# Diagonal blocks computed once, their decay and shift on GpSimd, and the attention result kept transposed

## The chip, the cores and the metric

The kernel runs on one core of a Trainium2 chip. The metric is the device time of one execution in microseconds (us); three runs before the change gave 2750.56, 2752.46 and 2753.69 us. Everything is computed in float32 or in sums of bf16 parts; the tensor engine has two clock levels, and a window of the profile shows the granted one as a share of full speed (1.00 or 0.50).

## The reference

The reference is one transformer block on x of 8 x 1024 x 256, with a modulated layer norm ahead of attention and ahead of the feed-forward part. Cut to what matters here:

```python
q, k, v = h @ W_q, h @ W_k, h @ W_v
latent = (k + v) @ W_down_kv                      # 64 wide
k_rec, v_rec = latent @ W_up_k, latent @ W_up_v   # 16 heads of 16
scores = einsum("bhqd,bhkd->bhqk", qh, k_rec) / sqrt(256)
scores = scores * exp(-0.01 * abs(t[:, None] - t[None, :]))
attn = softmax(scores)
x = x + ga * (einsum("bhqk,bhkd->bhqd", attn, v_rec) @ W_o)
h = layernorm(x) * (1 + cb) + sb
x = x + gb * fp4_linear(silu(fp4_linear(h, w_gate)) * fp4_linear(h, w_up), w_down)
```

fp4_linear rounds both operands, in blocks of 16, to a grid of eight magnitudes and multiplies.

## The kernel before

The kernel has five stages: a small setup, the projections, attention (lines 492 to 968), a setup of the feed-forward part, and the feed-forward part (lines 1137 to 1481). The change touches attention and the last stage.

**The decay.** The decay of the distance between query and key is split into two factors, one for the query's row and one for the key's, each with its own sign of the exponent. So there are two versions of the queries and keys: "low" serves keys at or behind the query in one direction, "up" the other. Each float32 value is held as three bf16 parts; a product of two such values is six products of parts, stacked along the contraction (96 rows), and three more rows carry the negated maximum of the query (KROWS 96, ROWS 99), so that a product comes out of TensorE already shifted for the exponential. In a block of 128x128 on the diagonal both versions are needed, each on its side.

**Units and steps.** A unit is one batch and four heads; there are 32. It has 16 steps g: half hf = g // 8 of the queries (512 of them) against key block kb = g % 8 (128 keys). Steps 0 to 3 and 12 to 15 hold the diagonal (`is_diagonal`). In a step TensorE computes, for each of four heads, one tile of 128 keys by 512 queries in one of two score banks (`scores`, L702 to L724), and between them the score tiles of a later unit whose row maxima VectorE takes (`max_tile` L681, `maxima` L850; the custom instruction at L856 multiplies by the decay and takes the maximum). ScalarE takes the exponential of each tile (L817). At the end of the step TensorE multiplies the probabilities of step g - 2 with the values, which have a column of ones for the sum (`values`, L738 to L752). A score bank is free when the exponential two tiles back is done.

**The diagonal before.** In a diagonal step the score tile's diagonal 128 columns come from the low version (L718), and a product of the identity with a mask of -2^100 (`unserved`, L719) takes away the wrong side. Behind the second head TensorE computes the four up blocks into side_ps (`up_diagonals`, L734). VectorE limits them with a mask (`limit_up`, L891), ScalarE takes their exponential in the next step (L821), and GpSimd adds them to the probabilities (`add_diagonal`, L651). TensorE's `values` of the step wait for that.

**The output before.** ScalarE copies the accumulated output out of PSUM (L812, at steps 1 and 9), TensorE turns it by four transposes (`turn_out`, L762, at steps 5 and 10), VectorE inverts the sums and multiplies (L914, L920), and GpSimd's queue stores it (L657).

**The maxima.** At steps 7 and 8 VectorE splits the maxima of the next unit into three parts (`split_maxima`, L860 to L876); TensorE turns them at step 9 (L699), VectorE copies them (L881), and SyncE writes them into the three extra rows of the queries (`load_max_rows`, six DMAs, L600).

**Queues.** SyncE runs in the order of `step` (L603 to L612): it waits until all exponentials of a unit are done (L607), then issues 24 loads of the low queries and keys two units on and the up ones of the next unit (L487), the values (L593), and, once the maxima are turned, their rows.

**The last stage** runs 64 tiles of 128 tokens through a software pipeline (L1143 to L1151): attention is loaded, turned by TensorE (`turn_attention`, L1266), copied by ScalarE together with the turned normed input (L1317), projected (L1239), normed, rounded, multiplied with gate and up (L1284), rounded again, turned, and multiplied down (L1249). GpSimd raises one column a tile to the power -0.5 there (L1362), as it does four columns a half batch in the projections (L339).

## Time and profile before

| what | us |
|---|---|
| median of three runs | 2752.46 |
| the profiled execution | 2753.01 |
| its span in the trace | 2751.1 |
| TensorE busy (share) | 2592.5 (94%) |
| VectorE busy | 2308.7 (84%) |
| ScalarE busy | 1600.6 (58%) |
| GpSimd busy | 971.2 (35%) |

The span is the stretch from the first to the last instruction in the trace; the execution's own time has 1.9 us around it. A busy time is the sum of the times in which the engine had an instruction running. Matmuls are pipelined, so the distance between the starts of two of them tells what one costs. Projections take about the first 350 us, attention the time from there to 2060, the last stage the time from 2105 on. The mean granted clock is 0.944.

### The profile page before, as it was taken

Reading aid. Unit: us, or ns where it says so; the run is one execution under the profiler, and the core shown is the slowest. Engines: PE = TensorE matmul, PEld = TensorE weight load, DVE = VectorE, ACT = ScalarE, POOL = GpSimd, SP = SyncE. Lnnn points to the kernel's source line nnn. Section 1 sums busy time; section 2 is a strip of 40 time slices with the busy share of each in tenths; the row PEclk is TensorE's granted clock in tenths of the full one; section 3 lists DMA queues with packets and bytes.
Section 4 is the critical chain, followed back from the end, with each engine's and each line's share of the span. In section 5 each row is a group of like instructions: output and inputs, shape, how many; then the busy total and the mean of one; then the engine's idle time right before and its main releaser. Section 6 shows DMA issues by size and latency. Waiting matters only on the chain. (4 is left out here: it accounts for less than half of the span.)

```text
span 2751.1 us, 44454 instructions
## 1 busy us (share of the span) xinstructions
PE 2592.5 (94%) x15110; PEld 1205.3 (44%) x15110; DVE 2308.7 (84%) x4659; ACT 1600.6 (58%) x2988; POOL 971.2 (35%) x865
## 2 busy tenths in 40 slices
PE   5787669999999999999999999999977999999998
PEld 3333304344344344344344344343323566666665
DVE  5988788888888888888888888888755888888886
ACT  3666507777777777777777777777762222222221
POOL 3666532222122122122122122122131565556664
PEclk9667659999999999999999999999996999999999
DMA  4778864546546536446446446456201111111110
GB/s 153 239 243 257 264 127 82 85 62 91 82 62 92 81 66 95 74 69 96 72 71 95 70 74 95 69 74 92 47 7 39 37 44 42 41 41 43 41 34 18
DMA packets 207074, 238.20 MB, mean 87 GB/s; under 512 B 32256, under 2 KB 150784, under 8 KB 206720
## 3 DMA queue, kind: packets, MB, share of 16 engines
q1 hardware_dynamic: 194560, 218.56, 41.2%
q0 software_dynamic: 3072, 8.39, 1.2%
q10 hardware_dynamic: 9216, 8.39, 0.9%
q8 instruction: 122, 2.00, 0.4%
q14 instruction: 104, 0.85, 0.1%
HBM read 149.79 MB, written 83.89 MB: 85 GB/s over the span
## 5 line engine op out<-in xcount | busy, mean ns | idle before, releaser
L856 DVE CUSTOM_DVE_ANT_0 unread<-max_ps,toeplitz_sb 128x1024 bf16<-128x1024 f32 x1024 | 1218.5, 1218 | 212.9 <-PE max_ps L689 207.6
L817 ACT ACTIVATE probs<-score_ps 128x512 f32<-128x512 f32 x2048 | 1111.5, 598 | 431.0 <-PE score_ps L722 287.3
L689 PE MATMUL max_ps<-k_low,q_low 96*128 96x512 bf16 x2048 | 712.9, 391 | 27.5 <-DVE ident_bf L847 17.9
L651 POOL TENSOR_TENSOR probs<-probs,up_probs 128x512 f32<-128x512 f32 x256 | 336.3, 1314 | 610.0 <-ACT up_probs L821 610.0
L750 PE MATMUL pv_ps<-probs,v 128*32 128x512 f32 x4096 | 545.5, 605 | 3.3 <-POOL probs L651 3.3
L714 PE MATMUL score_ps<-q_up,k_up 99*128 99x512 bf16 (+3 forms) x1280 | 408.6, 320 | 5.3 <-ACT probs L817 4.5
L722 PE MATMUL score_ps<-q_low,k_low 99*128 99x512 bf16 (+3 forms) x1280 | 406.2, 318 | 5.2 <-ACT probs L817 4.5
L1284 PE MATMUL gu_ps<-wgu_t,turned 128*128 128x512 f32 (+1 forms) x768 | 314.4, 559 | 0.6 <-DVE hid L1445 0.6
L657 POOL DMA_DIRECT2D attn<-out_n x64 | 48.8, 763 | 694.8 <-DVE out_n L920 671.4
L714 PEld LDWEIGHTS score_ps<-q_up,k_up 99*128 99x128 bf16 x1280 | 123.8, 97 | 357.3 <-ACT probs L817 340.8
L689 PEld LDWEIGHTS max_ps<-k_low,q_low 96*128 96x128 bf16 x2048 | 193.3, 99 | 146.0 <-DVE row_max L856 68.3
L719 PE MATMUL score_ps<-unserved,ident_bf 128*128 128x128 bf16 x1024 | 225.8, 220 | 0.0
L718 PE MATMUL score_ps<-q_low,k_low 99*128 99x128 bf16 x1024 | 224.7, 219 | 0.8 <-ACT probs L817 0.7
L346 POOL TENSOR_TENSOR parts<-rest,parts 128x512 bf16<-128x512 f32 x128 | 172.8, 1369 | 110.3 <-ACT parts L461 108.7
L1284 PEld LDWEIGHTS gu_ps<-wgu_t,turned 128*128 128x128 f32 x768 | 141.7, 191 | 141.0 <-issue 124.0
L722 PEld LDWEIGHTS score_ps<-q_low,k_low 99*128 99x128 bf16 x1280 | 126.0, 99 | 164.3 <-ACT probs L817 149.9
L1249 PE MATMUL fdown_ps<-wd_g,hid_t 128*128 128x256 f32 (+1 forms) x768 | 190.7, 390 | 4.6 <-DVE y_out L1459 3.4
L1324 ACT ACTIVATE silu<-gu_ps 128x704 f32<-128x704 f32 x64 | 48.6, 759 | 248.7 <-PE gu_ps L1284 248.7
L891 DVE TENSOR_TENSOR up_probs<-side_ps,up_limit 128x512 f32<-128x512 f32 x256 | 175.6, 686 | 13.8 <-PE side_ps L734 11.4
L1317 ACT ACTIVATE turned<-fturn_ps 128x512 f32<-128x512 f32 (+1 forms) x68 | 39.0, 573 | 233.8 <-PE fturn_ps L1274 221.8
L821 ACT ACTIVATE up_probs<-up_probs 128x512 f32<-128x512 f32 x256 | 162.1, 633 | 0.0
L1249 PEld LDWEIGHTS fdown_ps<-wd_g,hid_t 128*128 128x128 f32 (+1 forms) x768 | 141.3, 191 | 44.9 <-issue 26.3
(145 smaller groups left out, 3186.3 us busy)
## 6 DMA issues: line engine op xcount, KB each, us to landing
splits<-parts SPq DMA_DIRECT2D x128, 384.0 KB, 2.7
q_low<-splits SPq DMA_DIRECT2D x192, 128.0 KB, 4.4
k_low<-splits SPq DMA_DIRECT2D x192, 128.0 KB, 7.2
q_up<-splits SPq DMA_DIRECT2D x192, 128.0 KB, 9.8
k_up<-splits SPq DMA_DIRECT2D x192, 128.0 KB, 12.7
v_padded<-v_out SPq DMA_DIRECT2D x64, 256.0 KB, 3.7
v<-v_padded SPq DMA_DIRECT2D x32, 512.0 KB, 14.8
x_in<-in_L_attn_x SPq DMA_DIRECT2D x16, 512.0 KB, 5.3
```

What stands on the lines that cost most here:

```text
L651: nc.gpsimd.tensor_tensor(probs[:, g % PROBS, :, at:at + P], probs[:, g % PROBS, :, at:at + P], up_probs[:, g % 2], ALU.add).then_inc(diag ...
L689: mm = pe.matmul(max_ps[:, i % 2, half * HALF:(half + 1) * HALF], low[0][u][0:KROWS, h, qb * P:(qb + 1) * P], low[1][u][0:KROWS, h, half * ...
L714: mm = pe.matmul(score_ps[:, i % 2, 0:turn - q0], up[1][u % 2][:, h, ks], up[0][u % 2][:, h, q0:turn], start=True, stop=True)
L718: pe.matmul(at, low[1][u][:, h, ks], low[0][u][:, h, ks], start=True, stop=False)
L719: mm = pe.matmul(at, ident_bf[:], unserved[:], start=False, stop=True)
L722: mm = pe.matmul(score_ps[:, i % 2, turn - q0:HALF], low[1][u][:, h, ks], low[0][u][:, h, turn:q1], start=True, stop=True)
L750: mm = pe.matmul(pv_ps[h * VW:(h + 1) * VW, :], v[u][:, kb, h, :], probs[:, g % PROBS, h, :], start=(kb == 0), stop=(kb == TILES - 1))
L817: nc.scalar.activation(probs[:, g % PROBS, h, :], score_ps[:, i % 2, :], ACT.Exp).then_inc(exp_done, 1)
L856: nc.vector.tensor_tensor_reduce(unread[:, i % 2, :], max_ps[:, i % 2, :], toeplitz[:, at:at + S], 1.0, -3.0e38, ALU.mult, ALU.max, row_ma ...
L891: nc.vector.tensor_tensor(up_probs[:, g % 2], side_ps[:], up_limit[:].unsqueeze(1).broadcast_to([P, UH, P]), ALU.min).then_inc(up_limited, 1)
L1249: mm = pe.matmul(down_ps[:, 0:D], hid_t[i % 2][0:rows, c, :], w["wd_g"][0:rows, b, c, :], start=(c == 0), stop=(c == IC - 1))
L1284: mm = pe.matmul(gu_ps[:, c:min(c + HALF, GU)], turned[(i + TURN_INPUT) % 2][:, DC + k, :], w["wgu_t"][:, k, c:min(c + HALF, GU)], start=( ...
```

## The change

In attention each diagonal block is computed once, from the low version without the maximum rows, into side_ps, one step ahead of its own step (`diagonals`); the score tile leaves its 128 columns out. ScalarE copies the four blocks out (`copy_diagonal`), GpSimd multiplies them with a decay (`decay_diagonal`) and subtracts the query maxima (`shift_diagonal`), and ScalarE takes the exponential into the probabilities in the step after (`diagonal_exp`). The maxima for that are turned whole, in float32, beside the three parts, stored to DRAM and loaded back broadcast over the 128 partitions, 1 MB a half unit (`load_shift`). The mask, `limit_up`, `add_diagonal` and the up blocks go.

The values' padding columns are all ones, so 16 rows of the accumulated output hold the sum. It is not turned: SyncE copies these rows beside the output's by four DMAs (`move_sums`), GpSimd raises a tile of 128x512 to the power -1 and multiplies (`normalise`, both halves after the next unit's step 3), and SyncE stores it by four DMAs (`store_out`). The last stage loads it transposed and has no `turn_attention`. The values and the buffers of the weights' rounding share less memory than before.

```diff
@@ attention, SyncE
+        def load_shift(unit, hf):
+            sp.wait_ge(max_stored, 16 * (unit + 1))
+            if unit > 0:
+                sp.wait_ge(diag_shifted, 2 * DIAG * (unit - 1) + DIAG * (hf + 1))
+            sp.dma_start(shift[:, hf], t["max_whole"].rearrange("(h c) q -> h (c q)", c=TILES)[
+                :, hf * HALF:(hf + 1) * HALF].unsqueeze(0).broadcast_to([P, UH, HALF])).then_inc(shift_loaded[hf], 16)
+
+        def move_sums(unit, hf):
+            n = 2 * unit + hf
+            sp.wait_ge(out_copied, n + 1)
+            if unit > 0:
+                sp.wait_ge(out_normal, n - 1)
+            for h in range(UH):
+                sp.dma_start(inverse[h * VW:h * VW + HD, hf, :],
+                             out_t[h * VW + HD:(h + 1) * VW, n % OUTS, :]).then_inc(sums_moved[hf], 16)
+
+        def store_out(b, u, hf):
+            n = 2 * (UNITS * b + u) + hf
+            sp.wait_ge(out_normal, n + 1)
+            for h in range(UH):
+                sp.dma_start(t["attn_t"][b, u * UH + h, :, hf * HALF:(hf + 1) * HALF],
+                             out_t[h * VW:h * VW + HD, n % OUTS, :]).then_inc(out_stored[n % OUTS], 16)
         def step(b, u, last):
...
             if not (last and u == UNITS - 1):
                 load_up(b if u < UNITS - 1 else b + 1, (u + 1) % UNITS)
+            if unit > 0:
+                load_shift(unit, 1)
+                sp.wait_ge(pv_done, STEPS * unit)
+            if not (last and u == UNITS - 1):
+                load_v(b if u < UNITS - 1 else b + 1, (u + 1) % UNITS)
+            if unit > 0:
+                move_sums(unit - 1, 1)
+                store_out(*before, 0)
+                store_out(*before, 1)
+            move_sums(unit, 0)
+            if not (last and u == UNITS - 1):
                 load_max_rows(unit + 1, (u + 1) % UNITS)
+                load_shift(unit + 1, 0)
@@ attention, GpSimd
+        def decay_diagonal(unit, g):
+            n = diagonals_before(unit, g)
+            pool.wait_ge(diag_copied, n + 1)
...
+            nc.gpsimd.tensor_tensor(diag[:, g % 2], diag[:, g % 2], diag_decay[:].unsqueeze(1).broadcast_to([P, UH, P]),
+                                    ALU.mult).then_inc(diag_decayed, 1)
+
+        def shift_diagonal(unit, g):
+            n, hf, at = diagonals_before(unit, g), g // TILES, g % DIAG * P
+            pool.wait_ge(diag_decayed, n + 1)
+            pool.wait_ge(shift_loaded[hf], 16 * (unit + 1))
+            nc.gpsimd.tensor_tensor(diag[:, g % 2], diag[:, g % 2], shift[:, hf, :, at:at + P],
+                                    ALU.subtract).then_inc(diag_shifted, 1)
+
+        def normalise(unit, hf):
+            n = 2 * unit + hf
...
+            pool.wait_ge(sums_moved[hf], 16 * UH * (unit + 1))
+            nc.gpsimd.tensor_tensor(inverse[:, hf, :], inverse[:, hf, :], minus_one[:].broadcast_to([P, HALF]),
+                                    ALU.pow).then_inc(inverted, 1)
+            pool.wait_ge(inverted, n + 1)
+            nc.gpsimd.tensor_tensor(out_t[:, n % OUTS, :], out_t[:, n % OUTS, :], inverse[:, hf, :],
+                                    ALU.mult).then_inc(out_normal, 1)
+
+        def unit_steps(unit):
             for g in range(DIAG):
-                add_diagonal(b, u, g)
+                decay_diagonal(unit, g)
+                shift_diagonal(unit, g)
+            if unit > 0:
+                normalise(unit - 1, 0)
+                normalise(unit - 1, 1)
             for g in range(TILES + DIAG, STEPS):
-                add_diagonal(b, u, g)
+                decay_diagonal(unit, g)
+                shift_diagonal(unit, g)
@@ attention, TensorE
+            pe.transpose(turned_max, max_parts[:].rearrange("p t n -> p (t n)"), ident_bf[:])
+            pe.transpose(turned_whole, row_max[:, unit % 2], w["ident"][:]).then_inc(max_turn_ready, 1)
...
             if is_diagonal(g):
-                at = score_ps[:, i % 2, turn - q0:turn - q0 + P]
-                pe.matmul(at, low[1][u][:, h, ks], low[0][u][:, h, ks], start=True, stop=False)
-                mm = pe.matmul(at, ident_bf[:], unserved[:], start=False, stop=True)
                 turn += P
...
             for h in range(UH):
-                mm = pe.matmul(side_ps[:, h, :], up[1][u % 2][:, h, ks], up[0][u % 2][:, h, ks],
+                mm = pe.matmul(side_ps[:, h, :], low[1][u][0:KROWS, h, ks], low[0][u][0:KROWS, h, ks],
                                start=True, stop=True)
...
-                    if h == 1 and is_diagonal(g):
-                        up_diagonals(b, u, g)
+                    if h == 1 and is_diagonal((g + 1) % STEPS) and not (last and g == STEPS - 1):
+                        diagonals(*steps_on(b, u, g))
@@ attention, ScalarE
         def exp(unit, g, h):
             i = UH * g + h
+            first = P if is_diagonal(g) and g % DIAG == 0 else 0
+            end = HALF - P if is_diagonal(g) and g % DIAG == DIAG - 1 else HALF
...
+            nc.scalar.activation(diag[:, g % 2], side_ps[:], ACT.Copy).then_inc(diag_copied, 1)
...
+            act.wait_ge(diag_shifted, diagonals_before(unit, g + 1))
+            nc.scalar.activation(probs[:, g % PROBS, :, at:at + P], diag[:, g % 2], ACT.Exp).then_inc(diag_exp_done, 1)
...
                 for h in range(UH):
                     exp(unit, g, h)
-                    if h == UP_EXP and not (first and g == 0) and is_diagonal((g - 1) % STEPS):
-                        up_exps(*steps_back(b, u, g, 1))
+                    if h == DIAG_EXP and not (first and g == 0) and is_diagonal((g - 1) % STEPS):
+                        diagonal_exp(*steps_back(b, u, g, 1))
+                if is_diagonal((g + 1) % STEPS) and not (last and g == STEPS - 1):
+                    copy_diagonal(*steps_on(b, u, g))
@@ attention, VectorE: limit_up, invert_sums and normalise go; copy_turned copies the whole maxima too
+            nc.vector.tensor_copy(max_whole[:], turned_whole).then_inc(max_turn_copied, 1)
@@ last stage
-            sp.dma_start(attn_in[i % 4][:], t["attn"][b, i * P:(i + 1) * P, :]).then_inc(tile_loaded[i % 4], 16)
+            sp.dma_start(attn_in[i % 4][:], t["attn_t"][b, :, :, tokens].rearrange(
+                "(k h) d s -> (h d) k s", k=DC)).then_inc(tile_loaded[i % 4], 16)
...
-                mm = pe.matmul(out_ps[:, 0:D], turned[i % 2][:, k, :], w["wo_g"][:, b, k, :],
+                mm = pe.matmul(out_ps[:, 0:D], attn_in[i % 4][:, k, :], w["wo_g"][:, b, k, :],
```

## Rows read from the trace of the kernel before

**Rows 1.** Windows of attention and feed: busy us (count), PEclk, DMA share, GB/s

```profile
1000.00:1050.00 50.00, 50.00 (x374) 20.59 (x366) 43.36 (x81) 37.73 (x73) 11.79 (x10) 1.00 0.47 69
2300.00:2700.00 400.00, 399.90 (x1577) 257.26 (x1575) 354.42 (x995) 91.27 (x165) 241.18 (x249) 1.00 0.13 39
```

**Rows 2.** Timeline of the SyncE queue: start us, us, engine, line, operation

```profile
1012.23 1.78 SPq L600 DMA_DIRECT2D q_low<-max_turned  x3
...
1029.20 2.65 SPq L487 DMA_DIRECT2D q_low<-splits  x6
...
1040.34 0.43 SPq L593 DMA_DIRECT2D v<-v_padded  x1
...
1080.60 3.01 SPq L487 DMA_DIRECT2D q_low<-splits  x6
```

**Rows 3.** Timeline of TensorE in one unit

```profile
1005.62 1.07 PE L750 MATMUL pv_ps<-probs,v 128*32 128x512 f32 x8
...
1008.57 1.06 PE L750 MATMUL pv_ps<-probs,v 128*32 128x512 f32 x8
...
1012.65 0.66 PE L762 MATMUL side_ps<-ident_sb,out_t 128*128 128x128 f32 x4
1013.14 0.38 PE L722 MATMUL score_ps<-q_low,k_low 99*128 99x512 bf16 x1
...
1016.08 0.23 PE L718 MATMUL score_ps<-q_low,k_low 99*128 99x128 bf16 x1
1016.14 0.22 PE L719 MATMUL score_ps<-unserved,ident_bf 128*128 128x128 bf16 x1
...
1018.40 1.06 PE L750 MATMUL pv_ps<-probs,v 128*32 128x512 f32 x8
...
1021.73 1.06 PE L750 MATMUL pv_ps<-probs,v 128*32 128x512 f32 x8
```

**Rows 4.** Timeline of ScalarE in a diagonal step

```profile
1020.92 0.63 ACT L821 ACTIVATE up_probs<-up_probs 128x512 f32<-128x512 f32 x1
1021.44 1.09 ACT L817 ACTIVATE probs<-score_ps 128x512 f32<-128x512 f32 x2
```

**Rows 5.** GpSimd groups by form: count | busy us, mean ns | idle

```profile
L651 POOL TENSOR_TENSOR probs<-probs,up_probs 128x512 f32<-128x512 f32 x256 | 336.3, 1314 | 610.0 <-ACT up_probs L821 610.0
...
L1362 POOL TENSOR_TENSOR rstd<-var_eps,minus_half 128x1 f32<-128x1 f32 x64 | 42.4, 662 | 31.9 <-DVE var_eps L1421 31.9
...
L339 POOL TENSOR_TENSOR rstd<-var_eps,minus_half 128x4 f32<-128x4 f32 x16 | 16.2, 1010 | 20.9 <-DVE var_eps L274 20.8
```

**Rows 6.** Timeline of projection: GpSimd and VectorE

```profile
118.77 2.57 POOL L346 TENSOR_TENSOR parts<-rest,parts 128x512 bf16<-128x512 f32 x2
...
120.36 1.53 DVE L303 TENSOR_TENSOR rest<-full,parts 128x512 f32<-128x512 f32 x1
...
125.86 0.68 DVE L303 TENSOR_TENSOR rest<-full,parts 128x512 f32<-128x512 f32 x1
```

**Rows 7.** Windows at attention's start and under a unit's loads

```profile
404.00:410.00 6.00, 4.90 (x10) 0.66 (x10) 5.81 (x11) 0.00 (x0) 0.00 (x0) 0.50 1.06 336
419.00:422.00 3.00, 2.62 (x25) 1.58 (x26) 3.00 (x6) 2.79 (x6) 1.16 (x1) 1.00 1.07 219
1030.00:1050.00 20.00, 20.00 (x158) 8.85 (x155) 17.02 (x29) 15.96 (x32) 6.43 (x5) 1.00 1.08 147
```

**Rows 8.** Timeline of TensorE at the end of attention

```profile
2062.50 5.62 PE L1047 MATMUL wmod_ps<-wmod_hi,silu_c 128*8 128x512 f32 x8 [4.28 <-PEq L968]
```

**Rows 9.** Timeline of TensorE in a feed tile

```profile
2412.24 0.44 PE L1266 MATMUL fturn_ps<-ident_sb,attn_in 128*128 128x128 f32 x2
...
2412.52 0.38 PE L1274 MATMUL fturn_ps<-ident_sb,h 128*128 128x128 f32 x2
```

**Rows 10.** DMA issues: out<-in, queue, count, KB each, median us to landing

```profile
k_up<-splits SPq DMA_DIRECT2D x192, 128.0 KB, 12.7
...
q_low<-max_turned SPq DMA_DIRECT2D x96, 8.0 KB, 1.9
```

318 lines of the change are left out of this document (139 added, 179 removed).

## The prediction

> **What bounds the kernel now.** I read the windows first, then the queue and engine timelines of one attention unit, then the groups by form, the DMA issues and the end of the stage. Of 50 us in the middle of attention TensorE is busy for all 50 at full clock, ScalarE for 37.7, VectorE for 43.4, GpSimd for 11.8; in the feed stage TensorE is busy for 399.9 of 400 us and VectorE for 354.4 [rows 1]. So TensorE is the bound in both, and GpSimd has room in the first. The SyncE queue starts the loads of one unit at 1029.20 and of the next at 1080.60: a unit (one batch, four heads, 16 steps) takes 51.4 us, and there are 32, 1645 us in all [rows 2]. The matmuls on the values (L750) end each step, so their starts give its length: 1005.62 to 1008.57, 2.95 us, for a plain step, 1018.40 to 1021.73, 3.33 us, for a diagonal one [rows 3]. A unit has eight of each.
>
> **What TensorE gains in attention.** In a diagonal step each of four heads loses one 128-column product and the identity product with the mask; two such instructions start 0.06 us apart, 1016.08 and 1016.14 [rows 3]. 8 x 0.057 = 0.45 us, so 2.88 us are left. The four side products stay, one step earlier; over a unit that is nothing. The two turns of the output go, each 0.49 us (1012.65 to 1013.14) [rows 3]; the added turn of the whole maxima is one small instruction, taken at 0.1 us, between 0.06 and 0.3 of the rows there. But ScalarE gets a copy in each diagonal step beside four exponentials and the exponential of the diagonal. One of its 512-wide instructions follows another by 0.52 us (1020.92 to 1021.44) [rows 4]; six take 3.14 us. So steps 1, 2, 13 and 14 cost 3.14 us and are ScalarE's; in steps 0, 3, 12 and 15 the exponentials are 384 wide and 2.88 us stay (if width brought them nothing, +0.26 us each, 1 us a unit). Step 1 also holds a copy of the output, now uncovered: +0.4 us. Unit: 51.4 - (26.6 - 4 x 3.14 - 4 x 2.88) - 0.98 + 0.1 + 0.4 = 48.4 us, a gain of 3.0 us, 96 us over 32 units. VectorE only loses work (limits, reciprocals, products); it was no bound, so nothing is booked for it. On GpSimd the decay and the shift are two products of 512 columns, 1.31 us each [rows 5], for one before: 2.6 us inside a step of 2.9 to 3.1 us. They run between the copy at the end of the step before and the exponential in the step after, some 4 us later, so they are hidden while GpSimd is free.
>
> **The power.** This is the term that decides. Each unit raises two tiles of 128x512 to the power -1 on GpSimd, and no row has that form. The nearest rows are powers: one column takes 662 ns, four take 1010 ns (16 of these; 64 of the first) [rows 5]. VectorE's next instruction starts right behind them, so the ends are real. Three columns more cost 348 ns: 0.116 us a column. Drawn out, 512 columns take 0.66 + 511 x 0.116 = 59.9 us. From below, a power could run at the rate of the 128x512 product, 1.3 us. I take the power's own rows, 59.9 us: the same operation, and the cost grows with every column already between one and four. The extrapolation is long, and a loop that does many columns at a time would not show in four; that is the main doubt, and it is priced below.
>
> The Trainium skill, GPSIMD Engine Reference, section "Elementwise - side-by-side cycle accounting", gives about 2.6 cycles an element for a two-input operation. The product row agrees; the two power rows are far above it. By that rule the power would be an estimated 1.1 us and the whole sum that of rival A.
>
> With 59.9 us a unit is bound by GpSimd. It works in this order: diagonals 0 to 3, then power and product of the two halves of the unit before, then diagonals 12 to 15. The two powers and the product between them take 59.9 + 1.5 + 59.9 = 121.3 us. Steps 4 to 8 pass below them; step 13 waits on ScalarE for the diagonal exponential of step 12, and behind that exponential wait all others, the score banks they free, and TensorE. A second wait is added: the split of the maxima (L868 to L875, steps 8 and 9) reads two SBUF tiles on VectorE. In the projection stage a subtraction of that kind starts at 120.36 while two GpSimd subtractions run from 118.77 to 121.34; it takes 1.53 us where the one at 125.86 takes 0.68, and ends 0.6 us after them [rows 6]. So VectorE stands until the running GpSimd instruction ends. The first split gets in after the first power, the last one has a maximum tile (1.2 us) ahead of it and meets the second power. Behind it are the next maxima and TensorE's turn of them, so steps 10 and 11 come after the second power as well.
>
> The Trainium skill, SBUF - State Buffer, section "Who interferes with whom", says that such a VectorE instruction and a reading GpSimd instruction exclude each other for the whole instruction; by that rule, with which the trace agrees, the unit has the 5 us below. By a rule that lets them share it would have none.
>
> From the end of the second power to the start of the next first one: steps 10 and 11, 5.9 us; TensorE at half clock first, as after the stretch of gaps until 416, where 404 to 410 shows 0.50 and 419 to 422 shows 1.00 [rows 7], taken at 2 us; steps 12 to 15 and 0 to 3 of the next unit, 2 x 12.0 us; 0.6 us until the last shift ends: 32.5 us. Unit: 121.3 + 32.5 = 153.8 us. If the split slips in between, steps 10 and 11 are hidden, and the reload of the maxima is late instead: SyncE issues four stores, four moves of sums, six rows, one store and one load behind the second product, 15.6 us until the broadcast has landed (the terms stand under A), then 10 us to the last shift, 121.3 + 1.4 + 15.6 + 10 = 148 us. I take 153.8.
>
> Stage: unit 0 has no power, 48.4 us; 31 units x (153.8 - 51.4) = 3174 us; less 3.0 us for unit 0. The end: before, TensorE stands 4.3 us ahead of the next stage at 2062.50 [rows 8], with its last turn some 5 us. Now both halves of the last unit are left, 122 us, and stores, 4 us; less the 5 us: +119 us (some 2 us of the first power overlap the last step).
>
> **Feed.** The turn of attention goes: its two instructions start at 2412.24 and the next kind at 2412.52, 0.28 us on TensorE, which is the bound [rows 1, 9]; 64 tiles, 18 us. One stage less in the pipeline saves about 2 us in the filling. The loads become 512-byte pieces at a DMA share of 0.13 [rows 1], hidden. -20 us.
>
> Sum on the profiled execution: its own time is 2753.0 us (span 2751.1 and 1.9 around it), 0.5 us above the median of 2752.5. 2753 + 3174 - 3 + 119 - 20 = 6023 us. With 148 us a unit it is 5840. Its own range is 5700 to 6200 (the slope by 2% either way is 75 us; clock and order of waits the rest).
>
> **Rivals.** A: the power runs at a product's rate, with T = 1.3 us. Then another chain has the last word: SyncE. At a unit's start it issues 24 loads until +11.2 us [rows 2]; the last ones land 12.7 us after their issue [rows 10], so the queue is full until +24; the traffic moves at 147 GB/s there and at 336 with other shapes [rows 7]. A half of the broadcast maximum (1 MB) is 3.1 to 7.1 us, taken 4.7, the values 2, and the moved sums of the second half land at +31. Product, stores 1.8, sums 1.8, six rows 3.6 (1.78 for three [rows 2]), store of the maxima 0.5 and 2 to land (1.9 for a small one [rows 10]), broadcast 6: it is there at +47.5 + T. It is needed at 48.4 + 3.0 = 51.4, so below T = 4 us nothing is lost; above it the decay of step 12 is late as well, and the unit becomes 43.9 + T. It equals 51.4 at T = 7.5 us, 0.015 us a column: from there on the change loses. For it: the cost of starting (one column 0.66 us, far above 0.116) says that short powers may not show the loop's rate. Against it: an eighth of the slope is needed. 2753 - 96 + 5 - 20 = 2642 us; up to T = 7.5 it rises to 2750. If the broadcast takes its 7.1 us twice, 2 to 3 us a unit are lost and the gain is nearly gone.
> B: the loop overlaps columns, a quarter of the slope, T = 15 us. Unit 59 us, 31 x 7.6 = 236, end +33, feed -20: about 3000 us; with T from 8 to 35 us, 2760 to 4500. For it: as for A, with less asked. Against it: the three columns show no overlap.
>
> **Chances.** Forecast 0.48, A 0.25, B 0.24, in between A and B within 0.2% (5.5 us, about what a measurement of this kernel can tell from no change) 0.03. Faster 0.25, same 0.03, slower 0.72. The forecast and B together hold 0.72, so the range must reach to A: 2640 to 6200, and beside it the likeliest case's own, 5700 to 6200.
>
> **What would show it.** Right: a GpSimd row of 128x512 with the constant -1 near 60 us, 64 of them; TensorE idle for over half of attention behind ScalarE, that behind GpSimd; max_rest or max_parts rows of VectorE of tens of us; the SyncE loads some 150 us apart. The rows of the score product in diagonal steps without the mask, six ScalarE instructions in a diagonal step and 0.28 us less from tile to tile in the feed hold in every case. Wrong: powers under 7.5 us, with units of 48 us (A) or units that wait for the moved sums and the broadcast (B).

## The result, and the profile after

The changed kernel takes **7311.11 us** (median of four runs, 7307.19 to 7319.26) beside 2753.07 us for the kernel before on the same chip (2750.56 to 2755.26): a ratio of 2.656, 95% interval 2.652 to 2.661. The profiled execution took 7319.26 us, 7317.5 us of them its span. The forecast was 6023 us, with a range of 2640 to 6200 (5700 to 6200 for its likeliest case). The direction and the main mechanism, a unit bound by GpSimd's powers, came as forecast; the size did not.

The page after opens with each engine's busy time, the granted clock and the costliest groups. The row of L729 holds the powers, which the forecast had priced from [rows 5].

```profile
PE 2573.5 (35%) x12710; PEld 1064.2 (15%) x12710; DVE 2165.6 (30%) x4307; ACT 1663.3 (23%) x3240; POOL 6554.9 (90%) x1185
PE   7772222222222222222222222222222222206999
PEclk7676666565666666666666666666666666657999
L729 POOL TENSOR_TENSOR inverse_rows<-inverse_rows,minus_one 128x512 f32<-128x512 f32 x64 | 5242.6, 81916 | 7.0 <-issue 0.4
L889 ACT ACTIVATE probs<-diag 128x512 f32<-128x512 f32 x256 | 164.4, 642 | 4434.2 <-POOL diag L720 4434.0
L787 PE MATMUL score_ps<-q_up,k_up 99*128 99x512 bf16 (+3 forms) x1280 | 440.5, 346 | 4434.7 <-ACT probs L875 4433.9
```

Read the last three together. TensorE stands 4434 us behind ScalarE's exponentials (L875), ScalarE stands 4434 us behind GpSimd's shift of the diagonal (L720), and GpSimd is hardly ever idle: it spends 5243 us in 64 powers of 81.9 us.

The timeline of GpSimd shows one unit in order (start us, us, engine, line, operation):

```profile
2996.33 81.92 POOL L729 TENSOR_TENSOR inverse_rows<-inverse_rows,minus_one 128x512 f32<-128x512 f32 x1
3078.33 1.26 POOL L732 TENSOR_TENSOR out_t<-out_t,inverse_rows 128x512 f32<-128x512 f32 x1
3079.72 81.92 POOL L729 TENSOR_TENSOR inverse_rows<-inverse_rows,minus_one 128x512 f32<-128x512 f32 x1
...
3179.22 1.27 POOL L720 TENSOR_TENSOR diag<-diag,shift 128x512 f32<-128x512 f32 x1 [2.30 <-DMA shift<-max_whole_dram]
...
3188.90 81.92 POOL L729 TENSOR_TENSOR inverse_rows<-inverse_rows,minus_one 128x512 f32<-128x512 f32 x1
```

From one first power to the next are 192.6 us: 163.8 in the two powers, 1.3 in the product between them, and 27.3 from the end of the second to the next first. While the first one runs the other engines do what they can, for some 31 us, and stop. When TensorE starts again the granted clock is 0.50 (windows from 3163 to 3169), from 3175 on it is 1.00. Windows of the same unit (busy us with counts, PEclk, DMA share, GB/s):

```profile
3080.00:3160.00 80.00, 0.00 (x0) 0.00 (x0) 0.00 (x0) 0.00 (x0) 80.00 (x1) 0.50 0.01 2
3165.00:3189.00 24.00, 20.94 (x132) 7.98 (x133) 14.44 (x24) 19.51 (x41) 18.61 (x16) 0.84 0.71 160
```

### The profile page after: what moved, and what is told of

The parts are those of the page before. It is cut to its first block and busy times, and to the rows that moved or that the text cites. A ratio compares the mean times of both kernels' runs of the same rounds, so it can differ in the third digit from the quotient of the medians.

```text
span 7317.5 us, 40866 instructions
## 1 busy us (share of the span) xinstructions
PE 2573.5 (35%) x12710; PEld 1064.2 (15%) x12710; DVE 2165.6 (30%) x4307; ACT 1663.3 (23%) x3240; POOL 6554.9 (90%) x1185
## 5 line engine op out<-in xcount | busy, mean ns | idle before, releaser
L729 POOL TENSOR_TENSOR inverse_rows<-inverse_rows,minus_one 128x512 f32<-128x512 f32 x64 | 5242.6, 81916 | 7.0 <-issue 0.4
L787 PE MATMUL score_ps<-q_up,k_up 99*128 99x512 bf16 (+3 forms) x1280 | 440.5, 346 | 4434.7 <-ACT probs L875 4433.9
L889 ACT ACTIVATE probs<-diag 128x512 f32<-128x512 f32 x256 | 164.4, 642 | 4434.2 <-POOL diag L720 4434.0
L875 ACT ACTIVATE probs<-score_ps 128x512 f32<-128x512 f32 (+1 forms) x2048 | 1066.1, 575 | 273.5 <-PE score_ps L792 137.6
L763 PE MATMUL max_ps<-k_low,q_low 96*128 96x512 bf16 x2048 | 761.5, 414 | 27.4 <-DVE ident_bf L919 17.9
L820 PE MATMUL pv_ps<-probs,v 128*32 128x512 f32 x4096 | 580.2, 641 | 0.0
L713 POOL TENSOR_TENSOR diag<-diag,diag_decay 128x512 f32<-128x512 f32 x256 | 324.5, 1267 | 152.8 <-ACT diag L883 130.5
L720 POOL TENSOR_TENSOR diag<-diag,shift 128x512 f32<-128x512 f32 x256 | 325.4, 1271 | 119.5 <-DMA shift<-max_whole_dram 101.8
L883 ACT ACTIVATE diag<-side_ps 128x512 f32<-128x512 f32 x256 | 155.9, 609 | 73.9 <-PE side_ps L804 73.9
L303 DVE TENSOR_TENSOR rest<-full,parts 128x512 f32<-128x512 f32 x128 | 118.0, 932 | 17.2 <-ACT parts L454 11.1
```

The source lines that it names most:

```text
L713: nc.gpsimd.tensor_tensor(diag[:, g % 2], diag[:, g % 2], diag_decay[:].unsqueeze(1).broadcast_to([P, UH, P]), ALU.mult).then_inc(diag_dec ...
L720: nc.gpsimd.tensor_tensor(diag[:, g % 2], diag[:, g % 2], shift[:, hf, :, at:at + P], ALU.subtract).then_inc(diag_shifted, 1)
L729: nc.gpsimd.tensor_tensor(inverse[:, hf, :], inverse[:, hf, :], minus_one[:].broadcast_to([P, HALF]), ALU.pow).then_inc(inverted, 1)
L763: mm = pe.matmul(max_ps[:, i % 2, half * HALF:(half + 1) * HALF], low[0][u][0:KROWS, h, qb * P:(qb + 1) * P], low[1][u][0:KROWS, h, half * ...
L787: mm = pe.matmul(score_ps[:, i % 2, 0:turn - q0], up[1][u % 2][:, h, ks], up[0][u % 2][:, h, q0:turn], start=True, stop=True)
L820: mm = pe.matmul(pv_ps[h * VW:(h + 1) * VW, :], v[u % 2][:, kb, h, :], probs[:, g % PROBS, h, :], start=(kb == 0), stop=(kb == TILES - 1))
```

## The experiments

Thirteen kernels were run. "Before" in each comparison is the kernel before on the same chip, 2753 to 2756 us. e2, e4, e8, e10, e12 and e14 are single executions, the others medians of four or five. Line numbers of fences are those of the kernel named.

**e1_product.** A product stands where the power stood, with the same waits and DMAs; the inversion is left out.

```
-            nc.gpsimd.tensor_tensor(inverse[:, hf, :], inverse[:, hf, :], minus_one..., ALU.pow)
+            nc.gpsimd.tensor_tensor(inverse[:, hf, :], inverse[:, hf, :], minus_one..., ALU.mult)
```

> The changed kernel with the power -1 replaced by a product with the same constant (the inversion is left out; every wait, instruction count and DMA stays). Theory P (the 64 powers of 81.9 us are the whole loss, GpSimd's serial work): the row falls from 81.9 to about 1.3 us, a unit from 193 us to what the next chain allows, 48.4 to 51.4 us, and the time to 2640 to 2740 us; 64 x 80.6 = 5160 us less than 7311 would be 2150, which can't be reached, since 32 units at 48.4 are bound by TensorE and ScalarE. Rival Q (the SyncE chain, the rows and the broadcast of the maxima cost as much by themselves as was forecast for the powers' shadow): a unit stays above 54 us, TensorE idle behind max_rows or the shift, and the time is above 2830 us. Within P, 2642 us if the broadcast takes 4.7 us and the 24 loads leave the queue free by +24 us; near 2740 if the whole maxima and the row loads come 2 to 3 us late each unit.

Measured: 2659.5 us, ratio 0.965 (0.964 to 0.967). So all of the loss was the power's duration, and the rest of the change gains. The forecast had priced this case (rival A) at 2642 us; the product took 1.04 us in 62 of its 64 places.

**e2_half_width and e8_96_columns.** The same power over fewer columns; the other columns are not inverted.

```
-  inverse[:, hf, :], ... broadcast_to([P, HALF])
+  inverse[:, hf, 0:256], ... broadcast_to([P, 256])     (e8: 0:96, 96)
```

> The changed kernel with the power over 256 of the 512 columns of each half (the other columns are not inverted). Theory P: the power costs 0.160 us a column, so each takes about 41 us (a start of 0.5 us beside it), the unit falls by 2 x 41 to about 111 us, and the time to 7311 - 64 x 41 = about 4690 us. Rival: the cost is not in the columns (a fixed price of the instruction at this size, or a slow-down from what runs beside it): the row stays well above 41 us, and the time above 5000 us.

Measured: 4705 us, powers of 41.1 us, loads 112 us apart. The cost lies in the columns.

> The changed kernel with the power over 96 of the 512 columns of each half (the rest is not inverted): T = 0.16 x 96 = 15.5 us a power, the case that the forecast called B and priced at 3000 us (a unit of 43.9 + T = 59.4 us by the chain over SyncE). If that chain is right the unit is 59 to 60 us, the time 2753 - 96 + 31 x (59.4 - 48.4) + 33 = about 3030 us. Rival G (GpSimd's own series is the bound from the start: two powers, two products and the 27.3 us measured between the second power and the next first one): 2 x 15.5 + 1.3 + 27.3 = 59.6 us, the same time, but GpSimd never idle in the unit; if instead the two chains add (a power delays the products, these the stores and sums, and the sums the next power), the unit is over 62 us and the time over 3110 us. The idle time of GpSimd before the power and before the shift tells them apart.

Measured: 3075 us, powers of 15.62 us, and SyncE's first loads of a unit at 1070.79, 1132.41 and 1193.44, 61 to 62 us apart. GpSimd has 5.0 us of idle time in the unit looked at; the largest part is the shift that waits for the broadcast:

```profile
1132.95 1.27 POOL L713 TENSOR_TENSOR diag<-diag,diag_decay 128x512 f32<-128x512 f32 x1 [1.27 <-ACT diag L883]
1137.24 1.28 POOL L720 TENSOR_TENSOR diag<-diag,shift 128x512 f32<-128x512 f32 x1 [3.02 <-DMA shift<-max_whole_dram]
```

GpSimd's own series, 2 x 15.6 + 1.3 + 27.3 = 59.8 us, gives nearly all of the unit, and the chain over SyncE, by the 3.0 us before the shift, the rest: the time came out between the two cases that were written down (3030, over 3110).

**e4_bench and e12_powers.** Powers by themselves on GpSimd, ahead of attention in the kernel before.

```
+  for width, op, exponent in BENCH: nc.gpsimd.tensor_tensor(bench..., op)    (e4: 1 to 256 columns)
+  nc.gpsimd.tensor_tensor(...)  twenty times, one line each                  (e12)
```

> The kernel before with a list of instructions on GpSimd at the start of the attention stage: powers -1 of 1, 2, 4, 8, 16, 32, 64 and 256 columns (constant broadcast), powers -0.5 and -1 with and without a broadcast, products of 1 to 512 columns, one power over the decay table, and on VectorE fourteen additions or fewer of 128x512 with two SBUF inputs, three with GpSimd idle but for short powers, three while the power of 256 columns runs, six while products run. What is open: why 512 columns took 81.9 us when 1 and 4 columns of the kernel before (0.662 and 1.010 us) give 59.9. Theory K (a kink: the cost a column rises after the first few columns, for any exponent): 256 columns 41 us, 64 about 10.3, and the values up to 4 on the 0.116 line, -0.5 as dear as -1. Theory E (the exponent: -0.5 is cheaper than -1): 4 columns at -1 take 0.66 + 3 x 0.16 = 1.15 us or more, 64 columns at -0.5 about 8.0 and at -1 about 10.3. Theory V (the values): the powers of the constant 2 take another time a column than those of the decay table. For VectorE: if it stood for the whole GpSimd instruction, an addition started in the power of 256 columns would take up to 40 us; by the changed kernel's trace (0.18 to 0.19 us for the split of the maxima inside an 82 us power) it takes its usual time, about 0.7 us, up to 1.0, and beside products up to 1.5 us.

Measured, e4 (2850 us in all, as attention's start stands behind the list): at exponent -1, 64 columns 10.52 us and 256 columns 41.63; at -0.5, 4 and 64 columns take the same 1.01 and 10.52. Over the decay table 64 columns take 10.85. VectorE's 128x512 additions with two SBUF inputs took 0.69 us each beside powers of 2 to 8 columns, and 0.69, 0.98 and 0.69 us around the start of the power of 256. None waited for a power to end. Of the six beside products, four started inside a product of 512 columns, ended 0.55 us behind it and took 1.63 us; the first and the last, with no product under way at their start, took 0.69.

> The kernel before with a list of twenty single instructions on GpSimd at the start of the attention stage. Open is the row that bent the forecast's slope: in the kernel before a power of one column takes 0.662 us, in e4_bench 0.550 (exponent -1, value 2), while four columns take 1.008 to 1.010 in both. Theory V (values or exponent): one column at exponent -0.5 of 2, or of 0.001, takes 0.66 us and four of them 1.12 us or more. Theory N (what ran before it: the first power behind a product pays for a start): a power of one column behind a product takes 0.66 us and one behind a power 0.55 us, whatever the values. Theory S (steps: the cost goes by groups of columns): 1 and 2 columns, 3 and 4, 5 to 8 show steps and not a line. A power of 128 columns takes 20.6 to 20.9 us in every case.

Measured, e12 (2783 us in all): single instructions, each a line of its own (ns, start us, form). The first three are one column at -1 of 2, at -0.5 of 2, and at -0.5 behind a product; L676 and L680 are one column of 0.001 and of 700.

```profile
L648 POOL TENSOR_TENSOR bench<-bench x1: 549/549/549, 351.0 to 351.0; 128x1 f32<-128x1 f32 x1
L652 POOL TENSOR_TENSOR bench<-bench x1: 541/541/541, 352.2 to 352.2; 128x1 f32<-128x1 f32 x1
L656 POOL TENSOR_TENSOR bench<-bench x1: 546/546/546, 353.1 to 353.1; 128x1 f32<-128x1 f32 x1
L660 POOL TENSOR_TENSOR bench<-bench x1: 1013/1013/1013, 354.7 to 354.7; 128x4 f32<-128x4 f32 x1
L668 POOL TENSOR_TENSOR bench<-bench x1: 1636/1636/1636, 360.0 to 360.0; 128x8 f32<-128x8 f32 x1
L674 POOL TENSOR_TENSOR bench<-bench x1: 20722/20722/20722, 365.9 to 365.9; 128x128 f32<-128x128 f32 x1
L676 POOL TENSOR_TENSOR bench<-bench x1: 552/552/552, 386.7 to 386.7; 128x1 f32<-128x1 f32 x1
L680 POOL TENSOR_TENSOR bench<-bench x1: 556/556/556, 388.4 to 388.4; 128x1 f32<-128x1 f32 x1
```

A straight line: 0.55 us for the first column and 0.155 for each of the next seven (1636 - 549 over 7), 0.159 on to 128 and to 512 columns. Exponent, value and the instruction before change next to nothing, so theories V, N and S of that run fall, and so do K (no kink) and E (no dearer exponent) of e4. What is odd is the row that the forecast used for one column, 0.662 us.

**e14_feed_powers.** Two more powers behind the norm's in each feed tile.

```
             nc.gpsimd.tensor_tensor(rstd[:], var_eps[:], minus_half[:], ALU.pow)
+            nc.gpsimd.tensor_tensor(more_out[:, 0:4], more[:, 0:4], minus_half..., ALU.pow)
+            nc.gpsimd.tensor_tensor(more_out[:, 4:5], more[:, 0:1], minus_half..., ALU.pow)
```

> The kernel before with two more powers on GpSimd in each feed tile, right behind the one-column power of the norm: four columns and one column, of the constant 2 to the power -0.5. The forecast's slope came from a row of one column in the feed (mean 0.662 us, shortest 0.558) and one of four columns in the projections (1.010); alone, one column takes 0.549 to 0.556 us and each further one 0.155. Theory N (a neighbour: in the feed VectorE's instructions with two SBUF inputs start 0.16 us before the power and slow it a little): the norm's power stays at 0.66 us, four columns behind it take more than 1.01, 1.05 to 1.15 us, and the single column of the constant between 0.55 and 0.7, by what VectorE does beside it. Rival O (the operands: values out of the variance, or a tile of one column as exponent): the constant's single column takes 0.55 us and four take 1.01 in the feed as well, while the norm's stays at 0.66. The added 2 us a tile lie beside VectorE's and TensorE's work, so the time stays within 20 us of 2753.

Measured: 2757.8 us. Shortest, median and longest duration of each line:

```profile
L1364 POOL TENSOR_TENSOR rstd<-var_eps,minus_half x64: 559/660/662, 2111.7 to 2697.6; 128x1 f32<-128x1 f32 x64
L1366 POOL TENSOR_TENSOR more_out<-more,minus_half x64: 1009/1302/1304, 2112.3 to 2698.2; 128x4 f32<-128x4 f32 x64
L1369 POOL TENSOR_TENSOR more_out<-more,minus_half x64: 546/720/723, 2113.4 to 2699.6; 128x1 f32<-128x1 f32 x64
```

The same constant that takes 0.55 and 1.01 us alone takes 0.72 and 1.30 in the feed. So it is the place, not the operands: theory N holds in kind, though both times lie above its ranges (up to 0.7, up to 1.15). The timelines show which neighbour it is. In the kernel before, and then in this run:

```profile
2404.11 0.41 DVE L991 TENSOR_TENSOR h_buf<-h,h_scale 128x256 f32<-128x256 f32 x1
2404.27 0.66 POOL L1362 TENSOR_TENSOR rstd<-var_eps,minus_half 128x1 f32<-128x1 f32 x1 [0.37 <-DVE var_eps L1421]
```

```profile
2341.94 0.89 DVE L991 TENSOR_TENSOR hid_buf<-hid,hid_scale 128x704 f32<-128x704 f32 x1
2342.40 1.30 POOL L1366 TENSOR_TENSOR more_out<-more,minus_half 128x4 f32<-128x4 f32 x1
2343.58 0.52 DVE L995 TENSOR_SCALAR hid_buf<-hid_buf 128x704 f32<-128x704 f32 x1
2343.78 0.72 POOL L1369 TENSOR_TENSOR more_out<-more,minus_half 128x1 f32<-128x1 f32 x1
```

Each power starts while VectorE is inside an instruction that reads SBUF alone, and takes its own time plus what is left of that instruction, less 0.14 us: 0.25 left and 0.11 more, 0.42 left and 0.29 more, 0.32 left and 0.17 more. So it is for 185 of the 192 powers of this run, within 0.13 to 0.15 us, and for 62 of the 64 of L1362. In the first two tiles, where VectorE has little to do, the same lines take 1.01 to 1.02 and 0.55 to 0.56 us, and beside an instruction with an input in PSUM nothing is added (L339 of the kernel before, 14 of 16, with VectorE in L294). e4 has the same start in attention: 8 columns take 1.90 us with an addition under way and 1.64 alone (e12), and the 10.85 us over the decay table is such a start, not the table. The extra time is a wait at the start and does not grow with the columns; no run was made to take the neighbour away.

**e7_product_rows_first.** e1_product with SyncE's rows and broadcast of the maxima ahead of the eight stores.

```
             move_sums(unit - 1, 1)
-            store_out(*before, 0); store_out(*before, 1); move_sums(unit, 0)
             load_max_rows(unit + 1, ...); load_shift(unit + 1, 0)
+            store_out(*before, 0); store_out(*before, 1); move_sums(unit, 0)
```

> The changed kernel with a product in the place of the power (the inversion is left out), and SyncE's rows and broadcast ahead of the stores. In the run e1_product most units took 47.5 us and one of those looked at 55.0, with GpSimd's decay waiting 15 us for the diagonal's copy; 2659.5 us in all. Theory C (the chain over SyncE is what costs there, by stores that push the rows back now and then): the long units go, 32 x 47.5 = 1520 us of attention, and 2640 to 2650 us. Rival S (the long units are there for another reason, as a DMA ring that is full or ScalarE's order): no change from 2659 within 4 us.

Measured: 2642.4 us, ratio 0.959 (0.958 to 0.961), 17 us below e1_product. The queue of SyncE tells why. In e1_product:

```profile
1033.25 2.67 SPq L484 DMA_DIRECT2D q_low<-splits  x6
1080.70 2.71 SPq L484 DMA_DIRECT2D q_low<-splits  x6
1135.65 3.65 SPq L484 DMA_DIRECT2D q_low<-splits  x6
```

and in e7_product_rows_first:

```profile
1030.12 2.67 SPq L484 DMA_DIRECT2D q_low<-splits  x6
1077.55 2.67 SPq L484 DMA_DIRECT2D q_low<-splits  x6
1124.93 3.81 SPq L484 DMA_DIRECT2D q_low<-splits  x6
```

Behind the first three most units take 47.4 us in both; the single one of 55.0 us, and a few slightly long ones (the longest 51.3), are gone. The chain over the stores was real, but it decided only now and then.

**e10_turn_twice.** The kernel before with the feed's two attention turns made twice.

```
-            for k in range(DC):
+            for k in tuple(range(DC)) * 2:
                 mm = pe.transpose(turn_ps[...], attn_in[i % 4][...], w["ident"][:])
```

> The kernel before with the two 128-column turns of attention in each feed tile made twice (four instead of two; same result). The forecast booked 0.28 us a tile for taking them away, from start to start, 18 us in all, and the changed kernel showed 0.07 us a tile (9.615 to 9.54), 4.5 us in all. Theory F (fixed start: a group of turns behind the products of the hidden layer pays about 0.14 us once, whichever group comes first, so two turns are worth only what is left, 0.14 us): a tile takes 0.11 to 0.16 us more, 9.73 to 9.78 us, 7 to 10 us in all. Rival (each turn is worth what its start to start time says): +0.28 us, 9.90 us, 18 us in all. Rival 2 (TensorE has slack in the tile, as VectorE or a copy ends it): +0.07 us or less.

Measured: 2768.9 us. L1258 starts at 2407.22 and 2417.06, 9.84 us, beside 9.62 before: two more turns cost 0.22 us, between the theory's 0.16 and the rival's 0.28. Two turns taken away gave 0.08 (below). Both expectations missed.

**e5_reciprocal, e6_reciprocal_rows_first, e11_pieces, e13_sums_early.** The inversion on VectorE, to find whether the rest of the change can be kept. VectorE's `reciprocal` computes it. e5 puts one reciprocal of 128x512 for each half at the maxima of steps 9 and 11:

```
+        def invert(unit, hf):
+            dve.wait_ge(sums_moved[hf], 16 * UH * (unit + 1))
+            nc.vector.reciprocal(inverse[:, hf, :], inverse[:, hf, :]).then_inc(inverted, 1)
```

> The changed kernel with the inversion moved from GpSimd's power to VectorE's reciprocal of the same 128x512 tiles (64 of them, at the maxima of steps 9 and 11), the product stays on GpSimd; nothing else moves. Theory P: nothing but the power was wrong, so the diagonal scheme gains or loses what the rest allows. From the reciprocals of 16, 44 and 88 columns (0.230, 0.368, 0.695 us) 512 columns take 3.3 to 3.8 us, VectorE's unit is 41.8 + 0.6 + 7.2 = 49.6 us and becomes the bound or nearly so; the time is 2680 to 2760 us. Rival Q (the product comes at +38 us instead of +31, behind it stand eight stores, four moves of sums, six rows and the broadcast, 15.6 us, which is needed at +51.4): a unit of 53 to 56 us, TensorE idle behind the diagonal's decay or the rows of the maxima, and 2800 to 2900 us.

Measured: 3011.6 us, ratio 1.093 (1.091 to 1.094): worse than the rival's 2900. A reciprocal is 3.35 us; loads start at 1296.88 and 1356.36, 59.5 us apart, and the eight stores, held by the products, keep SyncE from 1337.15 to 1347.35, so the rows come at 1350.42.

e6: steps 5 and 9, and SyncE's order of e7.

```
-        INVERT_AT = ((9, 1), (11, 1))
+        INVERT_AT = ((5, 1), (9, 1))
```

> The changed kernel with VectorE's reciprocal in the place of the power (as in the run e5_reciprocal, 3.35 us each) but at the maxima of steps 5 and 9, and with SyncE issuing the rows and the broadcast of the maxima ahead of the eight stores instead of behind them. Theory C (e5_reciprocal lost 59.4 - 51.4 us a unit to the chain second reciprocal, products, stores 10.2 us, sums, rows, broadcast, shift): taken apart, the unit falls to the largest of the engines, VectorE with 32 x 1.30 + 0.6 + 2 x 3.35 + reads and gaps = 49 to 50 us, and the time to 2690 to 2720 us, faster than before. Rival V (VectorE is itself what costs in e5_reciprocal, since a late maximum delays TensorE): the unit stays above 53 us and the time above 2800 us.

Measured: 2838.3 us, ratio 1.030 (1.028 to 1.032), units of 54.6 us. Less than e5, but the rival came out, by its time and by its reason, a late maximum that delays TensorE. VectorE's total is not what costs: it was busy for 419 of 500 us. Windows around its first reciprocal (1077.38 to 1080.73):

```profile
1077.00:1079.00 2.00, 2.00 (x12) 0.66 (x14) 2.00 (x3) 1.67 (x4) 0.00 (x0) 1.00 1.10 149
1079.00:1081.00 2.00, 1.17 (x9) 0.10 (x1) 2.00 (x2) 1.09 (x3) 0.10 (x1) 1.00 1.05 171
1081.00:1083.00 2.00, 1.13 (x3) 0.28 (x3) 1.96 (x4) 0.06 (x1) 1.17 (x1) 0.70 1.05 350
1083.00:1085.00 2.00, 2.00 (x9) 0.59 (x9) 1.47 (x3) 1.14 (x2) 0.00 (x0) 0.50 1.03 387
```

TensorE runs out of free banks for the maxima (there are two) within 3 us, stands for 1.7 us (to 1081.87, behind row_max), and comes back at a granted clock of 0.50, 1.2 GHz. 47.4 + 2 x 3.35 = 54.1 us, nearly the unit that was measured: by the sum, each long VectorE instruction was paid in full.

e11 cuts each reciprocal of e6 into four pieces of 128 columns and moves the second half's product and stores behind the diagonals of steps 12 to 15.

```
+        INVERT_AT = ((1,1), (3,1), (5,1), (6,1), (9,1), (11,1), (12,1), (14,0))
-            nc.vector.reciprocal(inverse[:, hf, :], inverse[:, hf, :])
+            nc.vector.reciprocal(inverse[:, hf, cs], inverse[:, hf, cs])
```

> The run e6_reciprocal_rows_first (2838 us, unit 54.6) with each reciprocal cut into four of 128 columns, one each in steps 1, 3, 5, 6 (first half) and 9, 11, 12, 14 (second half), and the product of the second half behind the diagonals of steps 12 to 15. Theory B (a maximum has two score banks, so a VectorE instruction of 3.35 us stops TensorE, which is itself full and never makes it up: 47.4 + 2 x 3.35 = 54.1 us; VectorE was busy only 419 of 500 us): pieces of about 0.9 us meet the 0.48 us that VectorE waits in every step and the banks' own slack, the unit falls to 48 to 50 us and the time to 2660 to 2720 us. Rival V (VectorE's total is what costs): the total rises a little by the pieces' starts, no gain over 2838 us.

Measured: 2827.2 us, ratio 1.027 (1.024 to 1.030). A miss: the time is 11 us below e6's, close to what rival V said. The windows show another reason than the rival's:

```profile
1128.00:1132.00 4.00, 4.00 (x28) 1.16 (x21) 3.73 (x9) 2.85 (x6) 0.00 (x0) 1.00 1.06 208
1132.00:1136.00 4.00, 2.90 (x16) 0.66 (x14) 0.00 (x0) 2.81 (x6) 0.00 (x0) 1.00 0.75 272
1136.00:1140.00 4.00, 0.90 (x3) 0.28 (x3) 3.00 (x6) 0.00 (x0) 0.00 (x0) 0.67 0.00 0
1140.00:1144.00 4.00, 4.00 (x18) 1.11 (x16) 3.14 (x7) 2.28 (x4) 0.00 (x0) 0.50 0.06 12
```

VectorE (the third number) does nothing from 1132 to 1136: its piece, which starts at 1137.00, waits for moved sums that stand in the DMA queue behind 24 loads. TensorE stands with it for 4.2 us, up to 1139.10, and comes back at 0.50.

e13 issues them behind the first 12 loads and spaces the pieces out (shown against e11).

```
             load_low(...)
+            move_sums(unit - 1, 1)
             load_up(...)
-        INVERT_AT = ((1,1), (3,1), (5,1), (6,1), (9,1), (11,1), ...)
+        INVERT_AT = ((0,1), (2,1), (4,1), (6,0), (9,1), (11,0), ...)
```

> The run e11_pieces (2827 us, unit 53 to 55) with two moves. In e11_pieces VectorE reached the first piece of the second half at step 9 and stood until the moved sums landed, +31 us after the unit's first load, since they are issued behind 24 loads of 128 KB; TensorE stopped with it from 1133 to 1140 us and came back at a granted clock of 0.50 for some 4 us. Here SyncE issues the second half's sums behind the first 12 loads, and the pieces lie in steps 0, 2, 4, 6 and 9, 11, 12, 14. Theory B (a stop of VectorE longer than the two score banks cover, and the clock after it, is what the inversion costs there, and not VectorE's total): no stop is left, VectorE is busy for 39 + 8 x 0.95 = 46.6 us of a unit, the unit is 47.4 to 49 us and the time 2645 to 2700 us, faster than the kernel before. Rival V (VectorE's total, 46.6 of 47.4 us, leaves no room, and each piece of 0.95 us still delays TensorE by half of it): a unit of 51 us, 2755 us, no change from before.

Measured: **2692.9 us**, ratio 0.978 (0.977 to 0.979), with the whole computation. It beats both kernels, and it lies in theory B's range. Loads start 49.0 us apart (1103.18, 1152.22); VectorE is busy for 460 of 500 us, more than in e6, and no wait of TensorE for its maxima is longer than 0.6 us. So the stops were what cost, and not VectorE's total; what each of the two moves is worth was not run apart. The windows line and the row of the pieces:

```profile
1000.00:1500.00 500.00, 485.98 (x3134) 161.19 (x3132) 459.79 (x794) 417.65 (x840) 238.49 (x188) 1.00 0.70 130
L966 DVE RECIPROCAL inverse_rows<-inverse_rows 128x128 f32<-128x128 f32 x256 | 241.7, 946 | 27.9 <-DMA inverse_rows<-out_t 27.9
```

**e9_exp_of_log.** The inversion on ScalarE, with e7's order.

```
+  nc.scalar.activation(inverse[:, hf, :], inverse[:, hf, :], ACT.Ln)
+  nc.scalar.activation(inverse[:, hf, :], inverse[:, hf, :], ACT.Exp, scale=-1.0)
```

> The changed kernel with the inversion on ScalarE as exp(-log) (four instructions of 128x512 in steps 5, 6, 8 and 10 of a unit, none in a diagonal's crowded step) and SyncE's rows and broadcast ahead of the stores. ScalarE is busy for 385 of 500 us in e6_reciprocal_rows_first and one such instruction takes about 0.6 us. Theory I (any engine with room in its steps can invert for nothing; only the place of the work was wrong): the unit stays at the 47.4 us of e7_product_rows_first or up to 1 us above, and the time is 2642 to 2680 us, a version that beats both kernels. Rival T (the logarithm and the exponential need different tables, 1.28 us for each load by the row of the kernel before): four to eight loads a unit, 5 to 10 us, on an engine that bounds steps 1, 2, 13 and 14 and is near the bound in the others: 2800 to 3000 us.

Measured: 2875.4 us, ratio 1.045 (1.043 to 1.048). The rival holds: each of the 64 logarithms is preceded by a load of tables, and an exponential behind it by another.

```profile
L872 ACT ACT_TABLE_LOAD x64 | 82.1, 1283 | 1.1
L882 ACT ACT_TABLE_LOAD x63 | 80.8, 1283 | 1.1
```

That is 163 us by itself, of the 233 us above e7_product_rows_first; the 128 instructions themselves are 80 us of ScalarE.

## Why the prediction was wrong, step by step

**The power: the term that failed.** "Three columns more cost 348 ns: 0.116 us a column" took one row from the feed stage and one from the projections, and made a slope of their difference. The chip has 0.155 to 0.16. The four-column row was clean (1.010 us there, 1.013 alone in e12); the one-column row held 0.11 us of waiting for VectorE's instruction under way (0.662 in the feed, 0.55 alone; see e14). That wait is paid once for an instruction, whatever its columns. An error of 0.11 over three columns became 0.04 a column and 22.0 us over 512. The trace of before held the warning: the durations of L1362 run from 558 to 734 ns, and only the mean was read. With the shortest, (1008 - 558) / 3 = 0.150 a column and 0.56 + 511 x 0.150 = 77 us, close to 81.9. In the sum the error is 64 x 22.0 = 1408 us, 6023 + 1408 = 7431. The own range of 2% on the slope had no ground in the rows; the slope's own error was 27%.

The Trainium skill, GPSIMD Engine Reference, section "Elementwise - side-by-side cycle accounting", gives about 2.6 cycles an element, an estimated 1.1 us for 512 columns. That is right for the product that took the power's place in e1_product (1.04 us), and off by a factor of some 75 for the power at the same width (81.9 us).

**The second wait: not there.** The forecast had VectorE's split of the maxima stop for the second power, 32.5 us from its end to the next first one. The split ran inside the first power at its usual pace (VectorE's timeline; the power runs from 2996.33 to 3078.25):

```profile
3011.24 0.18 DVE L940 TENSOR_TENSOR max_rest<-row_max,max_parts 128x32 f32<-128x32 f32 x1
3011.34 0.18 DVE L942 TENSOR_TENSOR max_parts<-row_max,max_parts 128x32 bf16<-128x32 f32 x1
```

So steps 10 and 11 lie under the powers, and 27.3 us are left. Mean unit: the starts of the values' products run from 423.9 to 6463.5, (6039.6 - 48) / 31 = 193.3 us, where the forecast's form gives 197.8 with the true power: 31 x 4.5 = 140 us less. [Rows 6] was read too far: the wait beside a subtraction of 1.3 us was carried to a power 60 times as long. The row of 125.86, which served there as the undisturbed one, started inside a power of GpSimd and ended 0.10 us behind it, at its usual 0.68 us:

```profile
125.43 1.01 POOL L339 TENSOR_TENSOR rstd<-var_eps,minus_half 128x4 f32<-128x4 f32 x1 [1.59 <-DVE var_eps L274]
```

So the trace of before already held a power that did not stop VectorE. e4_bench shows both, 1.63 us for an addition that starts inside a product and 0.69 to 0.98 for one inside or just ahead of a power.

The Trainium skill, SBUF - State Buffer, section "Who interferes with whom", calls the port pair that the two engines share an exclusive lock, held by the first for its whole instruction. The additions behind products agree (they wait for the product's end), and so do the powers behind VectorE's instructions in e14. For VectorE behind a power no run here bears it out: 0.18 us inside one of 81.92.

**What TensorE gains: right, a little low.** Forecast 48.4 us a unit, measured 47.4 (e7_product_rows_first). A diagonal step is 2.86 us also where 3.14 was forecast, four times a unit, 1.1 us: ScalarE's copies and exponentials of score tiles follow each other by 0.48 us there (1178.17, 1178.65, 1179.13), and only the diagonal's exponential takes the 0.52 of [rows 4]. Attention's values run from 421.6 to 1939.6, 1518.0 us, beside 424.1 to 2056.3 before: 114 us gained, 96 forecast. Before, a unit took 1632.1 / 32 = 51.0 us on average, where the forecast went by one of 51.4.

**The chain over SyncE (rival A): right in kind.** 2642 us was forecast for a fast power, 2659.5 measured with SyncE's order as it is, 2642.4 with the rows ahead of the stores. That the last agrees to 1 us is luck: attention gained 18 us more than forecast and the rest 17 less. The moved sums land +32 us after a unit's first load, where +31 was worked out: in e11_pieces the first load is at 1104.86 and VectorE takes up its piece at 1137.00. The late broadcast shows in the changed kernel as well, 102 us of waits of the shift in 30 pieces.

**Rival B: priced too low.** "Unit 59 us" for T = 15 stands beside 61 to 62 measured at 15.6 (e8), 3000 beside 3075 us. It was priced by the chain over SyncE, 43.9 + T, a form that gives 47.9 at T = 4, where nothing was to be lost from 48.4. The forecast's own series of GpSimd would have said more, 2 x 15 + 1.5 + 32.5 = 64 us.

**The end: 159 us.** From the last values to the end of the span 854.0 us, before 694.8. The two powers of 81.9 us account for it: 119 - 20 + 2 x 22.0 = 143, and 16 more for the feed.

**Feed: some 13 us too good.** A tile was to lose 0.28 us [rows 9] and loses 0.08. TensorE's timeline after:

```profile
6988.69 0.44 PE L1306 MATMUL fturn_ps<-ident_sb,h 128*128 128x128 f32 x2
6989.05 0.88 PE L1298 MATMUL hid_ps<-ident_sb,hid 128*128 128x128 f32 x6
6989.77 4.89 PE L1316 MATMUL gu_ps<-wgu_t,turned 128*128 128x512 f32 x12
...
6998.23 0.44 PE L1306 MATMUL fturn_ps<-ident_sb,h 128*128 128x128 f32 x2
```

The group that now stands first (L1306 to L1298) takes 0.36 us where it took 0.22, and the hidden turns 0.72 where they took 0.65. Of the 0.28 us, 0.21 went to the groups behind. e10_turn_twice prices two turns in the middle at 0.22. Why the groups behind grow when a group ahead of them goes stays open.

Together, with 32 x 0.4 = 13 us for the unit of 51.0 that was taken as 51.4: 7431 - 140 + 13 + 16 = 7320 us, beside the profiled execution's 7319.3, for which the sum was made.

## What to carry to other kernels

A slope between two rows is only as good as the rows: take both from the same stage, read the shortest duration and not only the mean, look at what the other engine was running when the instruction started, and put the error of the difference, multiplied by the length of the extrapolation, into the range. Before work goes to an idle engine, ask for the longest single instruction and for what stands behind it there: with two buffers between engines, a 3.35 us instruction on an engine that is 84% busy cost its whole length (e6), and the same work in pieces of 0.95 us, spaced and with no stop for its data, cost a quarter (e13). When SyncE's queue carries stores that wait for late work, put what the next unit needs ahead of them.

## What the runs showed of the hardware

- A power on GpSimd is linear in the columns, 0.55 us for one and 0.155 to 0.16 for each further one up to 512, whatever the exponent (-1, -0.5); a product of 512 columns took 1.04 us alone (e4, e12, changed kernel).
- A power that starts while VectorE is inside an instruction on SBUF alone waits for what is left of it, less 0.13 to 0.15 us (e14: 0.72 for 0.55, 1.30 for 1.01 us); VectorE's maxima, which read PSUM, add nothing (the 64 powers of the changed kernel take 81.915 to 81.926 us, though these run beside some 30 us of a unit's first power and beside none of its second).
- VectorE's additions of 128x512 with two SBUF inputs: 0.69 to 0.98 us beside powers, 1.63 when started inside a product of 512 columns (e4).
- VectorE's reciprocal: 3.35 us for 512 columns, 0.95 for 128.
- After TensorE's stops of 1.7 us (e6) and 4.2 us (e11) the granted clock was 0.50 in the windows that follow (1083 to 1085, 1140 to 1144).
- A load of ScalarE's tables took 1.283 us, and logarithm and exponential in turn asked for one each (e9).
